# Score banks in pairs, one pair of banks for the maxima, and a new order of the matrix engine's step in a cross-attention kernel

## The chip, the core and the metric

The kernel runs on one core of a Trainium2 chip. The metric is the device time of one execution in microseconds. Engines are named as in the profile: PE (matmul), PEld (weight loads of PE), DVE (vector), ACT (scalar, activations), POOL (GpSimd) and SP (which issues most DMAs).

## The reference

Two layers of a gated network on x of 4 batches x 512 tokens x 512 features: a quantised linear pair (layer 0 attention slot), a mixture of 8 experts with top-2 routing and a shared expert, then a cross-attention with 32 heads of 16 features, and a second mixture of 8 experts. What matters here is the cross-attention and the routing:

```python
q = (x @ Wq).reshape(b, n, 32, 16);  k, v = split(ctx @ Wkv)      # per batch: 512 queries, 512 keys
q, k = rope(q, pos), rope(k, pos)
logits = einsum('bqhd,bkhd->bhqk', q, k) * 0.25
w = softmax(logits, axis=-1)
attn = einsum('bhqk,bkhd->bqhd', w, v)
return attn @ Wout + bout
# router of the first mixture
logits = xt @ gate_w.T          # 512 features to 8 experts
scores = softmax(logits);  top_k(scores + gate_b, 2)
```

## The kernel before

The program is a row of stages: the quantised pair with the keys, values and rotary tables beside it (0 to 297 us of the profile), the first mixture's router with its shared expert (299 to 448), its expert tiles (458 to 693), the attention (697 to 1382), the second mixture (to the end).

**Router.** Per batch, 4 matmuls over the feature chunks c accumulate the 8 x 512 logits in one PSUM bank (L803, 8 of the 128 columns of the array in use, float32: two records each), then four small transposes (L809). **Expert tiles.** `moe.tiles` tiles of 128 rows (40 here), each gathered, multiplied and stored, in a loop over groups of 8.

**Attention.** The work is in 16 units (b, c): batch b, chunk c of 8 heads. q and k are held as sums of bfloat16 parts, so that one bf16 matmul over 6 slots of 16 rows gives a product of float32 quality: Q6 and K6 hold 96 such rows for 8 heads, and three more rows (K: ones, Q: the parts of minus the row maximum) which subtract the maximum inside the score matmul. A turn of unit (b, c) has 8 steps; step s serves heads 4(s//4) to 4(s//4)+3 and key tile s%4. PE's step is written out by hand: `scores` (L1991) of heads 0 and 1, `maxima` (L2004), a slot for a job, `scores` of heads 2 and 3, `maxima`, `values` of the step before (L2016), another slot.

- `scores` writes one head's 128 keys x 512 queries to PSUM bank 4 or 5. `exps` on ACT (L2078) reads that bank and writes E; so a bank comes free for head h+2 after the exp of head h.
- `maxima` runs for a later unit (one or two units ahead): q x k for one head with queries on the partitions, two query tiles at a time, into banks 0, 1 or 2, 3 in turn. DVE reduces the two banks to the maxima `top` (L2217). A pair of banks is free again two pairs later: `pe.wait_ge(maxed, n_max(unit, h, pair) - 2)`.
- `values` takes four heads on four column groups of the array at once, V as weights, into bank 6.
- 16 slots per turn hold the jobs that use bank 7: q projection ("q"), x transposes ("x"), output projection ("p"), transposes of the maxima ("m", L1941), of the sums ("o", L1947) and of the attention rows ("a"). `jobs` gives the slots: q at 0, o at 4 and 11, a at 8, m at 10 of every unit; p and x in the turns c = 0 (slots 12 to 15) and c = 1 (slots 0 and 2).
- DVE runs its 16 reductions per turn, and after reduction n the tasks of slot n (statistics, normalisation, `cut_max` after 7, the shuffle of q after 2, the products of "o" and "p").
- The maxima of a unit go: DVE `cut_max`, PE "m", ACT copy to mT, POOL store to DRAM (L1912) and, when that has landed, POOL load into the three rows of Q6 (L1917); the first `scores` of the unit waits for this load.
- SP loads K6 with 6 DMAs (L1875), stores the parts of q, and loads Q6 with 6 DMAs (L1883). At the stage's start ACT fills the rows of ones with 4 copies (L2040).

Before unit 0 a prologue of turns with b = -1 does the first two q projections, then the maxima of unit 0 (16 reductions) and of half of unit 1 without scores beside them.

## Time and profile before

| | |
|---|---|
| median of 3 runs | 1527.67 us (1524.57 to 1527.68) |
| profiled execution | 1527.5 us, span 1526.0 us |
| PE busy | 1236.6 us (81%) |
| DVE busy | 845.2 us (55%) |
| ACT busy | 635.1 us (42%) |
| POOL busy | 392.8 us (26%) |
| mean granted clock | 0.905 |

Busy time is the time in which an engine had an instruction in work; it says nothing of which engine another waits for. The rows of the timeline and of the groups, further down, give that. A granted clock of 1.00 is the array's 2.4 GHz, 0.50 is 1.2 GHz.

### The profile page before, as it was taken

What the parts mean: (1) busy time and instruction counts of PE and PEld (TensorE: products, weight loads), DVE (VectorE), ACT (ScalarE), POOL (GpSimd) and SP (SyncE); (2) the same over time, 40 slices, a digit from 0 to 9 for tenths busy, and PEclk for the clock granted to TensorE, in tenths of its full rate; (3) what the DMA queues carried; (4) which work ended last, traced back from release to release, by engine and by line L of the source; (5) the groups of instructions that cost most, each with busy time, mean ns of one, the idle gap of its engine ahead of it and who ended that gap; (6) DMA issues with size and microseconds to landing.
All of it is one profiled execution on the core that took longest, in us unless ns stands there. A gap on an engine that the chain in (4) does not pass through costs nothing. (4 is left out here: it accounts for less than half of the span.)

```text
span 1526.0 us, 17989 instructions
## 1 busy us (share of the span) xinstructions
PE 1236.6 (81%) x5318; PEld 542.9 (36%) x5319; DVE 845.2 (55%) x1312; ACT 635.1 (42%) x1136; POOL 392.8 (26%) x459
## 2 busy tenths in 40 slices
PE   2757666499969999991376999999989999975897
PEld 2333333255534444440111323333333333222453
DVE  4585766631424555512385777766756776505544
ACT  1333232345532222224004565555645664742543
POOL 0505143201022222203632332222312330004332
PEclk8778787799999999996657999999999999997999
DMA  5142220243434444427384454433523541007001
GB/s 193 42 139 77 87 99 25 97 166 110 152 104 148 139 159 146 136 72 220 88 152 76 89 92 81 81 68 67 91 57 67 93 87 21 3 1 84 28 35 49
DMA packets 102990, 141.98 MB, mean 93 GB/s; under 512 B 17284, under 2 KB 72068, under 8 KB 102872
## 3 DMA queue, kind: packets, MB, share of 16 engines
q1 hardware_dynamic: 84984, 112.02, 29.2%
q0 software_dynamic: 17936, 29.11, 7.2%
q8 instruction: 34, 0.56, 0.2%
q14 instruction: 36, 0.29, 0.1%
HBM read 97.70 MB, written 46.53 MB: 95 GB/s over the span
## 5 line engine op out<-in xcount | busy, mean ns | idle before, releaser
L2217 DVE TENSOR_REDUCE a_top<-PS 128x2 f32<-128x1024 f32 x256 | 309.8, 1221 | 144.9 <-PE PS L2004 139.6
L2078 ACT ACTIVATE a_E<-PS 128x512 f32<-128x512 f32 x512 | 277.7, 596 | 156.8 <-PE PS L1991 155.4
L1991 PE MATMUL PS<-a_Q,a_K 99*128 99x512 bf16 x512 | 172.0, 388 | 37.3 <-ACT a_E L2078 13.9
L2004 PE MATMUL PS<-a_K,a_Q 96*128 96x512 bf16 x512 | 162.7, 402 | 31.2 <-DMA a_Q<-a_q_parts 19.1
L1252 PE MATMUL PS<-f_W,f_GT 128*128 x320 | 144.6, 595 | 0.0
L2016 PE MATMUL PS<-a_E,a_V 128*32 128x512 f32 x1024 | 139.6, 618 | 0.0
L1991 PEld LDWEIGHTS PS<-a_Q,a_K 99*128 99x128 bf16 x512 | 41.6, 97 | 205.3 <-ACT a_E L2078 164.5
L1323 DVE TENSOR_TENSOR f_H<-f_SG,PS 128x256 f32<-128x256 f32 x40 | 16.8, 421 | 129.7 <-ACT f_SG L1298 129.7
L2004 PEld LDWEIGHTS PS<-a_K,a_Q 96*128 96x128 bf16 x512 | 48.8, 100 | 91.6 <-DVE a_top L2217 27.4
L1252 PEld LDWEIGHTS PS<-f_W,f_GT 128*128 128x128 f32 x320 | 58.1, 192 | 58.2 <-issue 58.2
L1660 POOL TENSOR_TENSOR a_qf<-a_qf,a_tab 128x512 f32<-128x512 f32 x16 | 20.7, 1294 | 212.2 <-DVE a_swapped L2168 212.2
L1271 PE MATMUL PS<-f_W,f_HT 128*128 x160 | 75.1, 593 | 0.0
L1936 PE MATMUL PS<-a_xT,a_wq 128*128 128x512 f32 x128 | 64.1, 648 | 3.7 <-ACT a_xT L2051 3.0
L1957 PE MATMUL PS<-a_wo,a_attnT 128*128 128x512 f32 x128 | 60.4, 616 | 3.4 <-DVE X L2209 2.6
L1298 ACT ACTIVATE f_SG<-PS 128x256 f32<-128x256 f32 x40 | 15.4, 384 | 112.1 <-PE PS L1252 112.1
L2538 PE MATMUL PS<-f_W,f_xb 128*128 128x512 bf16 x256 | 61.9, 386 | 0.0
L825 PE MATMUL PS<-f_W,f0r_xT 128*128 128x512 f32 x128 | 58.3, 598 | 0.0
L1370 POOL DMA_INDIRECT a_rows<-f_y,l_pos x32 | 35.6, 1112 | 65.6 <-POOLq L54 40.2
L2328 POOL TENSOR_TENSOR f_H<-f_HF,f_gates 128x512 bf16<-128x512 f32 x32 | 33.4, 1045 | 71.5 <-DVE f_HF L2409 71.5
L1304 ACT COPY f_Y<-PS 128x512 f32<-128x512 f32 x40 | 23.5, 587 | 62.1 <-PE PS L1271 62.1
L1216 POOL DMA_INDIRECT f_G<-f_xn,f_idx x40 | 40.6, 1015 | 30.2 <-POOL f_idx L1213 30.2
L1213 POOL COPY f_idx<-f_token_of 128x1 int32 (+1 forms) x40 | 15.0, 374 | 128.5 <-PE PS L1232 121.3
(345 smaller groups left out, 1972.3 us busy)
## 6 DMA issues: line engine op xcount, KB each, us to landing
f0r_raw<-in_L_ffn_W_dram SPq DMA_DIRECT2D x24, 512.0 KB, 5.2
a_K<-k_parts SPq DMA_DIRECT2D x96, 128.0 KB, 4.9
a_Q<-a_q_parts SPq DMA_DIRECT2D x96, 128.0 KB, 4.5
f_y<-f_Y SPq DMA_DIRECT2D x40, 256.0 KB, 2.0
v_units<-V SPq DMA_DIRECT2D x16, 512.0 KB, 3.1
a_V<-v_units SPq DMA_DIRECT2D x16, 512.0 KB, 6.3
k_parts<-f_k_parts SPq DMA_DIRECT2D x16, 384.0 KB, 3.4
a_q_parts<-a_parts SPq DMA_DIRECT2D x16, 384.0 KB, 2.6
```

The lines of the kernel that those rows point to most:

```text
L825: last = nc.tensor.matmul(PS[:, 5, 0:2 * I], xT[b % 2][:, c, t * P:(t + 1) * P], W13[:, E, c, :], start=(c == 0), stop=(c == DC - 1))
L1216: pool.indirect_dma_start(out=G[k][:], out_offset=None, in_=xn_dram, in_offset=bass.IndirectOffsetOnAxis(ap=idx[:, k:k + 1].bitcast(U32), ...
L1252: last = nc.tensor.matmul(PS[:, 2 + k % 2, 0:2 * I], GT[k][:, c, :], W13[:, bass.ds(e, 1), c, :].rearrange("p a n -> p (a n)"), start=(c = ...
L1271: last = nc.tensor.matmul(PS[:, 6 + k % 2, :], HT[k][:, c, :], W2[:, bass.ds(e, 1), c, :].rearrange("p a n -> p (a n)"), start=(c == 0), s ...
L1936: last = nc.tensor.matmul(B, wq[:, d, c * P:(c + 1) * P], xT[:, d, :], start=(d == 0), stop=(d == DC - 1))
L1957: last = nc.tensor.matmul(B, attnT[:, d, extra * P:(extra + 1) * P], wo[:, d, :], start=(d == 0), stop=(d == DC - 1))
L1991: nc.tensor.matmul(PS[:, 4 + h % 2, :], K6[k][:, head, kt * P:(kt + 1) * P], Q6[k][:, head, :], start=True, stop=True).then_inc(st_done, 1)
L2004: last = nc.tensor.matmul(PS[:, t, :], Q6[k][0:KR, h, t * P:(t + 1) * P], K6[k][0:KR, h, :], start=True, stop=True)
L2016: last = nc.tensor.matmul(PS[32 * h:32 * h + 32, 6, :], V[k][:, kt, (step // 4) * 4 + h, :], E[step % 2][:, h, :], start=(kt == 0), stop=( ...
L2078: nc.scalar.activation(E[step % 2][:, h, :], PS[:, 4 + h % 2, :], ACT.Exp).then_inc(exp_done, 1)
L2217: nc.vector.tensor_reduce(top[:, h, 2 * pair:2 * pair + 2], PS[:, 2 * pair:2 * pair + 2, :], AX.X, ALU.max).then_inc(maxed, 1)
L2538: last = nc.tensor.matmul(PS[:, 2 * h + m, :], xb[b % 2][:, c, t * P:(t + 1) * P], W13[:, c, m, h * HE:(h + 1) * HE, :].rearrange("p e i - ...
```

## The change

Several edits are joined.

1. Q6 and K6 become [128, 2, 4, 512]: even heads (o = 0) keep slots in rows 0 to 95 and the three rows at 96; odd heads (o = 1) have slots 0 to 3 in rows 64 to 127, slots 4 and 5 in rows 0 to 31, the three rows at 32, and zeros in rows 35 to 63. Each load of K6, of Q6 and of the three rows is split in two (12, 12 and 2 DMAs for 6, 6 and 1). ACT fills the ones and the zeros with 16 instructions.
2. `maxima` uses only the first four slots, 64 rows, and takes two heads at once: even head on rows 0 to 63 into bank 0, odd head on rows 64 to 127 into bank 1. Every pair uses these two banks, and waits for the reduction just before it.
3. `scores` writes two heads to a pair of banks (2, 3 or 4, 5); one exp reads 128 x 1024. A pair of banks is free again a whole step later.
4. PE's step: scores of all four heads, `maxima`, slot, `values`, `maxima`, slot.
5. The first mixture's router puts the four chunks on four column groups (32 columns each) and adds them up in the turning matmul with a matrix `pick`.
6. `moe.tiles` is 39 instead of 40; the last group of the loop is written out.

```diff
-        self.tiles = -(-(2 * self.NT + experts - 1) // (2 * UNROLL)) * 2 * UNROLL
+        self.tiles = 2 * self.NT + experts - 1
...
+            for c in range(DC):
+                if c == 0:
+                    last = nc.vector.tensor_copy(pick[:], identf[:, 0:E])
...
                 for c in range(DC):
                     pe.wait_ge(xT_ready, b * DC + c + 1)
-                    last = nc.tensor.matmul(PS[0:E, 4, :], rwT[:, c, :], xT[b % 2][:, c, :], start=(c == 0), stop=(c == DC - 1))
+                    last = nc.tensor.matmul(PS[32 * c:32 * c + 32, 4, :], rwT[:, c, :], xT[b % 2][:, c, :], start=True, stop=True)
...
                 for i, part in enumerate(Q_PART):
-                    sp.dma_start(Q6[k][i * HEAD:(i + 1) * HEAD], q_parts[...]...).then_inc(q_loaded[k], 16)
+                    for o in range(2):
+                        at = ROWS[o][i]
+                        sp.dma_start(Q6[k][at.start:at.stop, o], by_head[o]).then_inc(q_loaded[k], 16)
...
-                    if not (is_first(unit) and step == 0 and h < 2):
-                        pe.wait_ge(exp_done, n_st(unit, step, h) - 2)
-                    nc.tensor.matmul(PS[:, 4 + h % 2, :], K6[k][:, head, kt * P:(kt + 1) * P], Q6[k][:, head, :],
-                                     start=True, stop=True).then_inc(st_done, 1)
+                    if not (is_first(unit) and step == 0):
+                        pe.wait_ge(exp_done, n_st(unit, step, pair) - 2)
+                    both = (step // 4) * 2 + pair
+                    for o, rows_ in enumerate((MAX_AT[0] + 3, P)):
+                        last = nc.tensor.matmul(PS[:, 2 + 2 * pair + o, :], K6[k][0:rows_, o, both, kt * P:(kt + 1) * P],
+                                                Q6[k][0:rows_, o, both, :], start=True, stop=True)
+                    last.then_inc(st_done, 1)
...
-                    if not (is_first(unit) and h == 0):
-                        pe.wait_ge(maxed, n_max(unit, h, pair) - 2)
-                    for t in range(2 * pair, 2 * pair + 2):
-                        last = nc.tensor.matmul(PS[:, t, :], Q6[k][0:KR, h, t * P:(t + 1) * P], K6[k][0:KR, h, :], start=True, stop=True)
+                    if not (is_first(unit) and h == 0 and pair == 0):
+                        pe.wait_ge(maxed, n_max(unit, h, pair) - 1)
+                    t = 2 * (h % 2) + pair
+                    for o in range(2):
+                        at = slice(o * FOUR, (o + 1) * FOUR)
+                        last = nc.tensor.matmul(PS[:, o, :], Q6[k][at, o, h // 2, t * P:(t + 1) * P], K6[k][at, o, h // 2, :],
+                                                start=True, stop=True)
                     last.then_inc(scored, 1)
...
                     scores((b, c), step, 0)
                     scores((b, c), step, 1)
                     maxima(*heads[step], 0)
                     slot(2 * step)
-                    scores((b, c), step, 2)
-                    scores((b, c), step, 3)
-                    maxima(*heads[step], 1)
                     if step == 0:
                         values(before(b, c, 1), 7)
                     else:
                         values((b, c), step - 1)
+                    maxima(*heads[step], 1)
                     slot(2 * step + 1)
...
-                    exps((b, c), step, (0, 1))
+                    exps((b, c), step, 0)
+                    exps((b, c), step, 1)
                     slot(2 * step)
-                    exps((b, c), step, (2, 3))
```

How this moves PE's instructions is seen best in steps 5 and 6 of a unit. PE before; L1991 are scores, L2004 maxima, L1941 the job "m", L2016 values, L1947 the job "o":

```order
L1991 MATMUL PS<-a_Q6_2,a_K6_2 128x512 x2
L2004 MATMUL PS<-a_K6_0,a_Q6_0 128x512 x2
L1941 MATMUL PS<-identb,a_mcut 24x128 x4
L1991 MATMUL PS<-a_Q6_2,a_K6_2 128x512 x2
L2004 MATMUL PS<-a_K6_0,a_Q6_0 128x512 x2
L2016 MATMUL PS<-a_E0,a_V2 32x512 x4
L1947 MATMUL PS<-identf,a_OT 128x128 x4
L1991 MATMUL PS<-a_Q6_2,a_K6_2 128x512 x2
```

PE of the changed kernel at the same place; L1986 are scores, L2004 again maxima, L1934 "m", L2017 values, L1940 "o":

```order
L1986 MATMUL PS<-a_Q6_2,a_K6_2 128x512 x4
L2004 MATMUL PS<-a_K6_0,a_Q6_0 128x512 x2
L1934 MATMUL PS<-identb,a_mcut 24x128 x4
L2017 MATMUL PS<-a_E0,a_V2 32x512 x4
L2004 MATMUL PS<-a_K6_0,a_Q6_0 128x512 x2
L1940 MATMUL PS<-identf,a_OT 128x128 x4
L1986 MATMUL PS<-a_Q6_2,a_K6_2 128x512 x4
```

The four scores stand together; the two pairs of maxima have only the values (and a job) between them on one side, and only the scores (and a job) on the other.

ACT at the start of the attention, before: the rows of ones, then the table load and the square root of the first normalisation (a_sd).

```order
L2040 COPY a_K6_0<-ones_b 3x4096
L2040 COPY a_K6_1<-ones_b 3x4096
L2040 COPY a_K6_2<-ones_b 3x4096
L2040 COPY a_K6_3<-ones_b 3x4096
L2092 ACT_TABLE_LOAD
L2092 ACTIVATE a_sd<-a_mv,ln_eps 128x4
```

ACT of the changed kernel: the first four of sixteen such rows; the same four follow for buffers 1, 2 and 3, and then the table load and a_sd.

```order
L2039 COPY a_K6_0<-ones_b 3x2048
L2042 ACTIVATE a_Q6_0<-ones_b 32x2048
L2042 ACTIVATE a_K6_0<-ones_b 32x2048
L2045 COPY a_K6_0<-ones_b 3x2048
L2039 COPY a_K6_1<-ones_b 3x2048
```

Four instructions of half the length took the place of each one.

## Rows read from the trace of the kernel before

**Rows 1.** Groups of instructions: busy us, mean ns | idle before, releaser.
```profile
L2217 DVE TENSOR_REDUCE a_top<-PS 128x2 f32<-128x1024 f32 x256 | 309.8, 1221 | 144.9 <-PE PS L2004 139.6
L2078 ACT ACTIVATE a_E<-PS 128x512 f32<-128x512 f32 x512 | 277.7, 596 | 156.8 <-PE PS L1991 155.4
...
L2203 DVE TENSOR_TENSOR a_attn<-PS,a_rsum 128x256 f32<-128x256 f32 x32 | 13.6, 424 | 1.3
```
**Rows 2.** Timeline of PE, one plain step: start us, length us, instruction, count, idle before.
```profile
1026.04 0.60 PE L1991 MATMUL PS<-a_Q,a_K 99*128 99x512 bf16 x2
1026.48 0.60 PE L2004 MATMUL PS<-a_K,a_Q 96*128 96x512 bf16 x2
...
1027.91 0.60 PE L2004 MATMUL PS<-a_K,a_Q 96*128 96x512 bf16 x2
1028.44 1.06 PE L2016 MATMUL PS<-a_E,a_V 128*32 128x512 f32 x8
1029.44 0.61 PE L1991 MATMUL PS<-a_Q,a_K 99*128 99x512 bf16 x2
...
1030.31 3.60 PE L1936 MATMUL PS<-a_xT,a_wq 128*128 128x512 f32 x8
```
**Rows 3.** Timeline of DVE: reduction 7, the one after `cut_max`, and two plain ones.
```profile
1014.28 1.23 DVE L2217 TENSOR_REDUCE a_top<-PS 128x2 f32<-128x1024 f32 x1 [0.20 <-PE PS L2004]
...
1016.74 2.35 DVE L2217 TENSOR_REDUCE a_top<-PS 128x2 f32<-128x1024 f32 x2
...
1027.12 1.22 DVE L2217 TENSOR_REDUCE a_top<-PS 128x2 f32<-128x1024 f32 x1 [0.74 <-PE PS L2004]
```
**Rows 4.** Timeline in the prologue, where PE waits for the reductions.
```profile
784.09 5.82 DVE L2217 TENSOR_REDUCE a_top<-PS 128x2 f32<-128x1024 f32 x5
...
785.35 0.60 PE L2004 MATMUL PS<-a_K,a_Q 96*128 96x512 bf16 x2 [1.14 <-DVE a_top L2217]
```
**Rows 5.** Timeline: first scores of three units, and POOL's load of the maxima.
```profile
946.87 0.60 PE L1991 MATMUL PS<-a_Q,a_K 99*128 99x512 bf16 x2 [0.31 <-DMA a_Q<-a_m_rows]
...
992.90 0.60 PE L1991 MATMUL PS<-a_Q,a_K 99*128 99x512 bf16 x2
...
1057.92 0.51 POOL L1917 DMA_DIRECT2D a_Q<-a_m_rows  x1 [4.92 <-DMA a_m_rows<-a_mT]
...
1061.57 0.60 PE L1991 MATMUL PS<-a_Q,a_K 99*128 99x512 bf16 x2 [1.15 <-DMA a_Q<-a_m_rows]
```
**Rows 6.** Timeline of PE in the last unit: two steps without maxima.
```profile
1332.02 0.88 PE L1991 MATMUL PS<-a_Q,a_K 99*128 99x512 bf16 x2 [0.47 <-ACT a_E L2078]
...
1334.90 0.88 PE L1991 MATMUL PS<-a_Q,a_K 99*128 99x512 bf16 x2 [0.47 <-ACT a_E L2078]
```
**Rows 7.** Timeline of the prologue: ACT's fills, its square root, SP's loads, DVE, first scores.
```profile
696.76 14.11 ACT L2040 COPY a_K<-ones_b 3x4096 bf16<-3x4096 bf16 x4 [3.31 <-PEq L54]
...
724.40 0.30 ACT L2092 ACTIVATE a_sd<-a_mv,ln_eps 128x4 f32<-128x4 f32 x1 [12.23 <-DVE a_mv L2139]
...
753.39 2.69 SPq L1883 DMA_DIRECT2D a_Q<-a_q_parts  x6
...
764.46 3.58 DVE L2217 TENSOR_REDUCE a_top<-PS 128x2 f32<-128x1024 f32 x3 [12.13 <-PE PS L2004]
...
789.94 0.20 DVE L2179 TENSOR_SCALAR a_ntop<-a_top 128x32 f32<-128x32 f32 x1
...
811.14 1.04 PE L1991 MATMUL PS<-a_Q,a_K 99*128 99x512 bf16 x2 [9.32 <-DMA a_Q<-a_m_rows]
```
**Rows 8.** Busy time by stretch: PE, PEld, DVE, ACT, POOL, granted clock, DMA share, GB/s.
```profile
766.00:769.00 3.00, 2.71 (x6) 0.26 (x4) 2.96 (x4) 0.00 (x0) 0.00 (x0) 0.50 1.04 313
...
1325.00:1350.00 25.00, 20.57 (x114) 5.55 (x113) 1.36 (x4) 20.07 (x39) 1.05 (x2) 1.00 0.01 3
```
**Rows 9.** The router's matmuls of the last batch (timeline); the expert tiles' first matmuls (line).
```profile
384.98 3.60 PE L803 MATMUL PS<-f0r_xT,f0r_rwT 128*8 128x512 f32 x8
...
L1252 PE MATMUL PS<-f_W,f_GT x320: 592/592/1061, 460.5 to 686.6; 128*128 x160
```

More of the change, by code:

```diff
@@ L678, in add @@
                     nc.vector.tensor_tensor(X[:, j, :], X[:, j, :], Z[j % TB][:], ALU.add).then_inc(added, 1)
+            for c in range(DC):
+                if c == 0:
+                    last = nc.vector.tensor_copy(pick[:], identf[:, 0:E])
+                else:
+                    v.wait_ge(pick_ready, c)
+                    last = nc.vector.tensor_tensor(pick[:], pick[:], identf[:, c * 32:c * 32 + E], ALU.add)
+                last.then_inc(pick_ready, 1)
             for b in range(NB):
@@ L807, in logit @@
                 pe.wait_ge(lT_ready, b + 1)
+                pe.wait_ge(pick_ready, DC)
                 for t in range(TB):
-                    last = nc.tensor.transpose(PS[:, 4, t * E:(t + 1) * E], lT[:, t * P:(t + 1) * P], identf[0:E, 0:E])
+                    last = nc.tensor.matmul(PS[:, 4, t * E:(t + 1) * E], lT[:, t * P:(t + 1) * P], pick[:], start=True, stop=True)
                 last.then_inc(l_turned, 1)
@@ L1142, in expert_tiles @@
         GT = [sb(f"GT{k}", [P, DC, P], dt) for k in range(U)]
-        H13 = [sb(f"H13_{k}", [P, 2 * I], dt) for k in range(U)] if narrow else None
         SG = [sb(f"SG{k}", [P, I], dt) for k in range(U)]
@@ L1183, in peeled @@
                     turn(group, i, lambda lag: 0 <= group * G + i - lag < T)
-            def looped(first, end):
-                with eng.Fori(first, end) as group:
-                    for i in range(G):
-                        turn(group, i, lambda lag: True)
+            assert T // G >= key_work.NB
             peeled(0, G)
-            if beside:
-                looped(1, key_work.NB)
-                for group in range(key_work.NB, T // G):
-                    peeled(group, G)
-            else:
-                looped(1, T // G)
-            peeled(T // G, deepest)
+            with eng.Fori(1, T // G) as group:
+                for i in range(G):
+                    turn(group, i, lambda lag: True)
+            peeled(T // G, T % G + deepest)
         def nth(j, k, unit):
@@ L1222, in _ @@
         def _(pe):
-            tb = 1 if dt == F32 else 2
             def turn_x(j, k):
@@ L1834, in n_max, with n_st @@
             return b * (DC * HU * 2) + c * HU * 2 + h * 2 + pair + 1
-        def n_st(unit, step, h):
+        def n_st(unit, step, pair):
             b, c = unit
-            return b * (DC * 32) + c * 32 + step * 4 + h + 1
+            return b * (DC * 16) + c * 16 + step * 2 + pair + 1
         block = s.enter_context(nc.Block())
@@ L1915, in turn @@
                     pool.wait_ge(pv_done, n_unit(unit, 8) - RING * 8)
+                else:
+                    pool.wait_ge(ones_ready, 4 * RING)
                 pool.nop(nofuse=True)
-                pool.dma_start(Q6[unit[1]][KR:KR + 3], row.rearrange("a (i h) s -> i (a h) s", i=3)).then_inc(m_loaded, 16)
+                by_head = row.rearrange("a (i h o) s -> o i (a h) s", i=3, o=2)
+                for o in range(2):
+                    pool.dma_start(Q6[unit[1]][MAX_AT[o]:MAX_AT[o] + 3, o], by_head[o]).then_inc(m_loaded, 16)
             turns(pool, turn)
```

150 lines of the change are left out of this document (75 added, 75 removed).

## Prediction

> **What bounds the kernel now.** I read the groups of instructions first, then the timeline of one plain step on PE and DVE, then the starts of units, the prologue and the tail. The groups [rows 1] show two engines that seem to wait for PE: DVE, 309.8 us of reductions with 144.9 us of idle time before them, and ACT, 277.7 us of exps with 156.8. Neither is full. In the plain step [rows 2] scores begin at 1026.04 and again at 1029.44: 3.40 us. Of this PE streams 4 scores and 4 maxima of about 0.22 each and the values, 1.00 (1028.44 to 1029.44), some 2.75; the rest are its waits for an exp before the second pair of scores. So the loop between two score banks and ACT costs about 0.6 us a plain step, and the double-buffered maxima cost nothing.
>
> **The half-step after the change.** Four banks let the exps run a step behind: PE no longer waits for them. But now every pair of maxima waits for the reduction just before it, and that reduction waits for its matmuls. The loop has four pieces. (a) From the first matmul of a pair to the reduction: 1026.48 to 1027.12, 0.64 [rows 2, 3], with two matmuls behind each other; if the two run side by side, 0.22 less, 0.43. (b) The reduction, 1.22 [rows 1]. (c) From its end to the next matmul: the reduction that starts at 784.09 ends at 785.31, PE starts at 785.35 [rows 4]: 0.04. (d) nothing else. Sum 1.70 per half-step, 3.40 per step. PE's own work between is smaller: maxima 0.22, a gap of 0.09 (values start 0.53 behind the maxima, where two matmuls take 0.44), values 1.00, together 1.3; on the other side 0.22 + 0.09 + four scores 0.87 + 0.09, about 1.3. So a plain step takes 3.40 after as before: **the bound moves from the exps to the reductions, and the step gains nothing.** PE's 0.4 us of slack per half hides short transposes (0.44); the long projection (3.44, from 1030.31 [rows 2]) makes its half 4.85, DVE standing idle meanwhile.
>
> That the halves run side by side is an assumption with bounds: the nearest row is the values, whose four matmuls of 32 columns take 1.00 together [rows 2] while the projection's four full ones take 3.44. The loop has 0.43 or 0.64 in it; I take 0.43. The Trainium skill (TensorEngine Tiling (Array Packing), Tiling Modes) says the same of row groups of 64, and also that a change of tiling mode drains the array, which speaks against this change: maxima in a mode of their own make four changes a step instead of two. The row prices one change at 0.09; by it the two added ones lie in halves that have 0.4 us of slack, so they cost nothing; were that slack absent, 2 x 0.09 x 128 steps would be 23 us.
>
> **What the loop costs in a unit.** Before, a vector task between reductions was hidden by the second pair of banks. Now it delays the next reduction by its length less 0.48 (the refill). cut_max: reduction 7 ends at 1015.51, the next starts at 1016.74 [rows 3], 1.23, so +0.75. The two "o" tasks (0.42 [rows 1] and a reciprocal, about 0.7 with their gaps) +0.25 each, the shuffle (estimate 0.75) +0.3, transposes that overflow the slack +0.15: 1.7 per unit. A unit of chunk 2 or 3 is then 4.85 + 15 x 1.70 + 1.7 = 32.05. Before: 1029.44 [rows 2] to 1061.57 less its wait of 1.15 [rows 5], 30.98. So **+1.1**. Chunk 1 with its three short jobs, two projections: 7.8 + 1.7 + 4.85 + 13 x 1.70 + 1.4 = 37.9, against 992.90 to 1029.44 [rows 5, 2], 36.5: **+1.4**. Chunk 0, with three output projections: 4.85 + 11 x 1.70 + 4.85 + 1.70 + 4.85 + 6.15 + delays 4.6 (statistics and normalisation too, an estimate) = 45.7, against 946.87 to 992.90, 46.0: **-0.3**; there PE's wait for ACT's table loads goes.
>
> **The maxima's transfer.** The chain m, copy, store, load is already late: scores at 1061.57 waited 1.15 us, at 946.87 0.31 [rows 5]. It now has less time. From the job in slot 10 to the next unit's scores: before 9.9 us, after 1.4 + 1.95 + 3 x 1.70 + 0.3 = 8.75, and 0.4 of lateness hides in the loop: 0.75 less. And it is longer: a second load on POOL behind the first (0.51 [rows 5]), and mT's copy behind both exps (0.25). So 1.5 us later in chunk 2 and 3, 0.3 after chunk 1, none after chunk 0 where projections cover it. Sum per batch: 3.3. With the units above, 2 x 1.1 + 1.4 - 0.3 + 3.3 = 6.6; rounded down, since batches differ, **+6.2 for each of batches 0, 1, 2**. Batch 0 also adds rows on DVE in each unit (1.5 us, an estimate, hidden before): 4 x 1.0, **+4**. Batch 3: three of its units lose 4 in all.
>
> **The tail.** 12 steps have no maxima. They take 2.88 now, with 0.47 waiting for an exp [rows 6]. After, an exp of 1024 elements bounds it: between 0.60 (no more than one of 512) and 1.19 (two of 596 [rows 1]); I take 1.0, nearer the two, since the elements stay and only one start is saved. PE's values stand between the scores, so the cycle is about 2.1: 12 x 0.75, some -9, of which 3.5 goes back to the maxima's transfer of the last unit, for which 2.5 short steps are too few: **-5**. The Trainium skill (ScalarE: Activation LUTs, What ACT_TABLE_LOAD costs) gives 186 ns + 0.833 ns an element less an overlap of 93, 0.95; by it the tail is 0.5 us shorter. Batch 3 together: **-1**.
>
> **The prologue** [rows 7]. Four fills took 14.11; sixteen of half the length take about 29.6 (3.53 halved, and a little more for the fixed part). The square root behind them began at 724.40, as its input came; now the fills end at 726.4 and a table load of about 1.3 follows: **+3.6** for everything to the first maxima. SP's Q6 loads: 2.69 for six, 5.4 for twelve, last data **+2**. Then 16 reductions stand between 764.46 and 789.94: 25.5, of which 16 x 1.16 [rows 4] is theirs. The clock is at 1.2 GHz there [rows 8], a single matmul takes 0.6 (1.04 for two, less 0.43), so a half is 0.61 + 0.04 + 1.22 + 0.05 = 1.92: 30.7 instead of 18.6, less about 1 hidden: **+11**. The job m stands three maxima later: **+1.6**. From m to the first scores at 811.14 took 16.7 us, because 2 MB of other loads share the DMA engines; they now come at another time: **-4**. Sum +14.2.
>
> **Before the attention.** Each router group of matmuls took 3.60 [rows 9]; on four column groups it should take what the values take, 1.06: 4 x 2.54, less DVE's four small pick instructions at the start (0.6, an estimate from the smallest vector rows, 0.2 as at 789.94 [rows 7], in a chain): **-9.6**; PE is full after, so this counts. One tile of 40 goes: (686.6 - 460.5)/40 [rows 9], **-5.7**.
>
> **Sum.** -9.6 - 5.7 + 14.2 + 3 x 6.2 + 4 - 1 = +20.5 on the profiled execution's 1527.5 (the median of the runs is 1527.67, the same): **1548 us**.
>
> **Rivals.** *The last unit's gain everywhere, the other side:* the loop is shorter than my four pieces say, because PE has its weights loaded and the release comes before the reduction's recorded end. It decides at a half-step of 1.61: some 230 halves are bound by the loop, 0.1 us on each is 23 us. At 1.60, with the transfer covered by the slack thus regained, 1548 - 23 - 10 = 1515. For it: DVE and PE rows are rounded and their ends modelled. Against it: the distances in [rows 3, 4] are between recorded starts. Chance 0.16. *The pairs of maxima don't overlap* (the change doesn't do what it says): 0.21 x 230 = +48, 1596. Chance 0.10. *The clock falls.* PE streams 2.2 of 3.4 us where it streamed 2.75. In the prologue 2.71 busy of 3.00 stood at 0.50; in the tail 20.57 of 25 kept 1.00 [rows 8], and there the streaming share is 1.87 of 2.88, 65%, as in the new step. That speaks for 1.00. At 1.2 GHz a half is PE's 2.5 us: 0.8 x a third of 230, +60, 1608. Chance 0.08. *It cancels:* the prologue's +14 hides in DMA waits and the time is 1527. Chance 0.06.
>
> **How the numbers follow.** A measurement tells 0.2%, 3 us, from no change. The forecast, 0.60, spans 1532 to 1565 for its unknown prices: exp, fills, transfer. The range takes most of both outer rivals: 1518 to 1592. Faster 0.16, within 0.2% 0.07 (the cancelling case and the edge of my own), slower 0.77.
>
> **What would show it.** Right: reductions 1.70 apart in plain halves, with idle time before the maxima ending in the reduction; almost no idle time before scores from an exp; first scores some 14 us later relative to the stage's start; waits of 2 to 3 us for the load of maxima before units of chunk 3 and 0; router matmuls of about 1 us. Wrong: plain steps well under 3.3 us, or reductions 1.9 apart, or a granted clock under 0.95 in the units.

## The result, and the profile after

The changed kernel takes **1537.82 us** (median of 4 runs, 1537.13 to 1539.43) against 1527.34 (4 runs, 1524.57 to 1527.68): ratio 1.0074, 95% interval 1.0057 to 1.0092, so 10.5 us slower. The forecast was 1548.0, with a range of 1518 to 1592. The profiled execution took 1538.25 us, with a span of 1536.8 beside 1526.0.

The page of the changed kernel, groups of instructions (busy us, mean ns | idle before, releaser) and DMA issues (count, KB each, us to landing):

```profile
L2223 DVE TENSOR_REDUCE a_top<-PS 128x2 f32<-128x1024 f32 x256 | 313.5, 1225 | 172.5 <-PE PS L2004 168.1
L2082 ACT ACTIVATE a_E<-PS 128x1024 f32<-128x1024 f32 x256 | 248.2, 1022 | 167.8 <-PE PS L1986 114.8
L2004 PE MATMUL PS<-a_K,a_Q 64*128 64x512 bf16 x512 | 105.6, 409 | 122.5 <-DVE a_top L2223 102.3
...
a_K<-k_parts SPq DMA_DIRECT2D x192, 64.0 KB, 2.2
a_Q<-a_q_parts SPq DMA_DIRECT2D x192, 64.0 KB, 2.2
```

Beside [rows 1] the reductions are as long as before (1225 ns against 1221), but DVE is idle for 172.5 us ahead of them instead of 144.9. The exps are half as many and cost 30 us less, on an engine that was not the bound. PE now idles 102.3 us ahead of maxima, for a reduction. The last two rows were not forecast: a load of 128 KB took 4.9 us (K) and 4.5 (Q) to land before; each of the two halves takes 2.2.

PE and DVE over three halves and the start of a unit of chunk 2 (compare [rows 2, 3]):

```profile
1031.26 0.39 PE L2004 MATMUL PS<-a_K,a_Q 64*128 64x512 bf16 x2 [0.52 <-DVE a_top L2223]
1031.59 1.04 PE L1986 MATMUL PS<-a_Q,a_K 99*128 99x512 bf16 x3
1032.98 0.39 PE L2004 MATMUL PS<-a_K,a_Q 64*128 64x512 bf16 x2 [0.35 <-DVE a_top L2223]
1033.30 1.07 PE L2017 MATMUL PS<-a_E,a_V 128*32 128x512 f32 x8
1034.69 0.39 PE L2004 MATMUL PS<-a_K,a_Q 64*128 64x512 bf16 x2 [0.33 <-DVE a_top L2223]
1035.02 1.05 PE L1986 MATMUL PS<-a_Q,a_K 99*128 99x512 bf16 x4
1036.41 0.39 PE L2004 MATMUL PS<-a_K,a_Q 64*128 64x512 bf16 x2 [0.34 <-DVE a_top L2223]
```
```profile
1033.41 1.23 DVE L2223 TENSOR_REDUCE a_top<-PS 128x2 f32<-128x1024 f32 x1 [0.49 <-PE PS L2004]
1035.13 1.23 DVE L2223 TENSOR_REDUCE a_top<-PS 128x2 f32<-128x1024 f32 x1 [0.49 <-PE PS L2004]
1036.84 1.23 DVE L2223 TENSOR_REDUCE a_top<-PS 128x2 f32<-128x1024 f32 x1 [0.49 <-PE PS L2004]
```

Maxima start 1.71 to 1.72 us apart, each pair behind the reduction before it: 0.43 from the matmul to the reduction (1036.41 to 1036.84), 1.22 of reduction, 0.06 back. Two matmuls on two row groups take 0.39 together, as one does, so they run side by side. In these plain halves DVE idles 0.49 and PE 0.33 to 0.35. There is no wait for an exp in these rows.

Where the time went, by marks that both traces have (us):

| stretch | before | after | difference | forecast |
|---|---|---|---|---|
| start to the first expert matmul | 460.5 | 454.0 | -6.5 | -9.6 |
| expert tiles | 226.1 | 221.4 | -4.7 | -5.7 |
| to the first transposes of x | 40.4 | 44.7 | +4.3 | +3.6 |
| to the first scores | 84.1 | 87.2 | +3.1 | +10.6 |
| batch 0 | 135.7 | 140.7 | +5.0 | +10.2 |
| batch 1 | 146.1 | 151.0 | +4.9 | +6.2 |
| batch 2 | 144.9 | 149.9 | +5.0 | +6.2 |
| batch 3, to the start of its last output projection | 139.9 | 136.0 | -3.9 | -1 |
| second mixture (not touched) | 148.2 | 152.0 | +3.9 | 0 |

The last row belongs to neither kernel. It is counted from the start of the last output projection. From the start of the last matmul of that projection the code is the same in all kernels here; counted so, the profile of before shows 145.1 us, after 148.9, and the twelve experiments 146.6 to 148.7. The granted clock tells them apart. Busy time by stretch (PE, PEld, DVE, ACT, POOL, granted clock, DMA share, GB/s), the same place in before and after:

```profile
1441.00:1461.00 20.00, 18.11 (x108) 9.50 (x109) 9.29 (x18) 9.83 (x15) 7.75 (x9) 1.00 0.08 27
```
```profile
1448.00:1468.00 20.00, 17.47 (x97) 8.93 (x99) 9.40 (x18) 9.84 (x15) 7.18 (x9) 0.91 0.08 28
```

Before has 1.00 there, after 0.91. So it is in all fourteen profiles: the five with 145.1 to 147.3 us show 1.00 in this stretch, the nine with 147.9 to 148.9 show 0.91, whatever their attention. Over the whole mixture the granted clock was 0.93 in before and 0.88 in after. It follows none of the edits. Whether it differs between executions of one kernel is not shown, since each kernel has one profile; but one profile of each is no ground for 3 us in a stretch that nothing changed.

### The profile page after: what moved, and what is told of

The parts are those of the page before. It is cut to its first block and busy times, and to the rows that moved or that the text cites. A ratio compares the mean times of both kernels' runs of the same rounds, so it can differ in the third digit from the quotient of the medians.

```text
span 1536.8 us, 17627 instructions
## 1 busy us (share of the span) xinstructions
PE 1179.3 (77%) x5253; PEld 520.2 (34%) x5317; DVE 846.6 (55%) x1314; ACT 626.6 (41%) x889; POOL 400.6 (26%) x474
## 5 line engine op out<-in xcount | busy, mean ns | idle before, releaser
L2223 DVE TENSOR_REDUCE a_top<-PS 128x2 f32<-128x1024 f32 x256 | 313.5, 1225 | 172.5 <-PE PS L2004 168.1
L2082 ACT ACTIVATE a_E<-PS 128x1024 f32<-128x1024 f32 x256 | 248.2, 1022 | 167.8 <-PE PS L1986 114.8
L2004 PE MATMUL PS<-a_K,a_Q 64*128 64x512 bf16 x512 | 105.6, 409 | 122.5 <-DVE a_top L2223 102.3
L2017 PE MATMUL PS<-a_E,a_V 128*32 128x512 f32 x1024 | 139.2, 611 | 0.4 <-ACT a_E L2082 0.4
L1986 PE MATMUL PS<-a_Q,a_K 128*128 128x512 bf16 (+1 forms) x469 | 131.9, 384 | 4.1 <-DMA a_Q<-a_m_rows 0.9
L2004 PEld LDWEIGHTS PS<-a_K,a_Q 64*128 64x128 bf16 x512 | 25.0, 93 | 294.3 <-DVE a_top L2223 247.4
L1929 PE MATMUL PS<-a_xT,a_wq 128*128 128x512 f32 x128 | 69.8, 695 | 3.7 <-ACT a_xT L2056 3.0
L1986 PEld LDWEIGHTS PS<-a_Q,a_K 99*128 99x128 bf16 (+1 forms) x512 | 41.4, 98 | 64.2 <-issue 23.1
L1901 POOL DMA_DIRECT2D a_m_rows<-a_mT x16 | 9.2, 577 | 165.8 <-ACT a_mT L2067 165.8
L2062 ACT ACTIVATE a_qf<-PS 128x512 f32<-128x512 f32 x16 | 9.6, 598 | 97.2 <-PE PS L1929 86.9
```

The costliest lines, as they stand in the source:

```text
L1929: last = nc.tensor.matmul(B, wq[:, d, c * P:(c + 1) * P], xT[:, d, :], start=(d == 0), stop=(d == DC - 1))
L1986: last = nc.tensor.matmul(PS[:, 2 + 2 * pair + o, :], K6[k][0:rows_, o, both, kt * P:(kt + 1) * P], Q6[k][0:rows_, o, both, :], start=True ...
L2004: last = nc.tensor.matmul(PS[:, o, :], Q6[k][at, o, h // 2, t * P:(t + 1) * P], K6[k][at, o, h // 2, :], start=True, stop=True)
L2017: last = nc.tensor.matmul(PS[32 * h:32 * h + 32, 6, :], V[k][:, kt, (step // 4) * 4 + h, :], E[step % 2][:, h, :], start=(kt == 0), stop=( ...
L2082: nc.scalar.activation(E[step % 2][:, 2 * pair:2 * pair + 2, :], PS[:, 2 + 2 * pair:4 + 2 * pair, :], ACT.Exp).then_inc(exp_done, 1)
L2223: nc.vector.tensor_reduce(top[:, h - h % 2:h - h % 2 + 2, t], PS[:, 0:2, :], AX.X, ALU.max).then_inc(maxed, 1)
```

## The experiments

Times are medians; a ratio is to the kernel before on the same chip, with its 95% interval. The experiments ran on several chips, on which the kernel before took 1526.0 to 1528.6 us, so a difference between two experiments can be a few us off.

**Router and tiles alone** (e6): the changed kernel with the attention of before.

```diff
-        def n_st(unit, step, pair):
+        def n_st(unit, step, h):
...
                     slot(2 * step)
+                    scores((b, c), step, 2)
+                    scores((b, c), step, 3)
+                    maxima(*heads[step], 1)
                     if step == 0:
...
-                    maxima(*heads[step], 1)
                     slot(2 * step + 1)
```

> The changed kernel with its attention put back to that of before: the router on column groups and 39 tiles stay. My accounting of the two traces says that these parts brought 6.5 us before the experts and 4.7 us in the tiles, so the time is 11.2 us under before: ratio 0.9927. It also tells what the 3.9 us in the second mixture are, whose code the change does not touch. If they come with the changed attention (its lower share of streaming matmuls, or an earlier end of its work on another engine), the second mixture takes 148.2 us here as before, and the granted clock in its first 20 us is that of before. Rival: they come with the shift in time or with the shorter tiles; then the mixture takes about 152 us here too and the gain is 7 us, ratio 0.995.

Measured: 1518.2 us, ratio 0.9945 (0.9932 to 0.9958), 8.4 us under before by the ratio, 9.4 by the medians. The tiles take 221.6 us, -4.5. The first expert matmul comes at 456.5. Over all profiles it comes at 458.0 to 460.5 with the old router (4 profiles, mean 459.3) and at 453.4 to 456.5 with the new (10, mean 454.6): the router brings 4.7 us, and the 6.5 of the table were partly chance. The second mixture took 150.4 us from the start of the last output projection, between the two theories (148.2 and 152): 2.2 of the 3.9 are there without the changed attention. So these two parts brought some 8 to 9 us and **the attention costs about 19**.

The router was forecast by the row of the values (1.06 for four column groups). Timeline of PE in the changed kernel, the router's matmuls of the last batch and what follows:

```profile
380.34 2.14 PE L814 MATMUL PS<-f0r_xT,f0r_rwT 128*32 128x512 f32 x8
382.42 3.70 PE L837 MATMUL PS<-f_W,f0r_xT 128*128 128x512 f32 x8
```

2.08 us from one to the other, where [rows 9] had 3.53: -1.45 for each of four batches, 5.8. Each matmul waits for its own copy of x, made by ACT in 0.60; whether that spacing keeps the four from running together was not tried.

**Two banks for the maxima in the kernel before** (e7).

```diff
-                    if not (is_first(unit) and h == 0):
-                        pe.wait_ge(maxed, n_max(unit, h, pair) - 2)
+                    if not (is_first(unit) and h == 0 and pair == 0):
+                        pe.wait_ge(maxed, n_max(unit, h, pair) - 1)
-                        last = nc.tensor.matmul(PS[:, t, :], ...
+                        last = nc.tensor.matmul(PS[:, t - 2 * pair, :], ...
-                        ... PS[:, 2 * pair:2 * pair + 2, :], AX.X, ALU.max)
+                        ... PS[:, 0:2, :], AX.X, ALU.max)
```

> The kernel before with one thing changed: the maxima go through two PSUM banks instead of four, so that each pair of matmuls waits for the reduction of the pair before. By my loop (0.64 from the first of two matmuls behind each other to the reduction, 1.22 reduction, 0.04 back) a half takes 1.90 and a plain step 3.80 instead of 3.40: over some 112 plain steps 45 us, with the tasks of VectorE no longer hidden some 10 to 15 more: ratio 1.036 to 1.040. This is also the case 'the pairs do not overlap' of my forecast with the old exps. Rival: the loop is shorter than its pieces, since the matmuls are issued ahead and the exps set the pace; then the plain step stays at 3.4 and the ratio is under 1.01.

Measured: 1587.88 us, ratio 1.0394 (1.0374 to 1.0413). Timeline of PE:

```profile
1058.94 0.60 PE L2004 MATMUL PS<-a_K,a_Q 96*128 96x512 bf16 x2
1059.65 0.88 PE L1991 MATMUL PS<-a_Q,a_K 99*128 99x512 bf16 x2
1060.86 0.60 PE L2004 MATMUL PS<-a_K,a_Q 96*128 96x512 bf16 x2 [0.32 <-DVE a_top L2217]
1061.39 1.07 PE L2016 MATMUL PS<-a_E,a_V 128*32 128x512 f32 x8
1062.39 0.61 PE L1991 MATMUL PS<-a_Q,a_K 99*128 99x512 bf16 x2
1062.83 0.60 PE L2004 MATMUL PS<-a_K,a_Q 96*128 96x512 bf16 x2
```

1.92 and 1.97 a half, 3.89 a step (1058.94 to 1062.83) against 3.80 by the sum of the pieces. This is the cost of one pair of banks without the pairing of matmuls: +60 us, from an edit of the banks alone. The rival with the shorter loop falls.

**The banks given back** (e2): changed kernel, four maxima banks and two score banks with one exp a head, PE's order of before; row groups, split loads and fills stay.

```diff
-                    if not (is_first(unit) and h == 0 and pair == 0):
-                        pe.wait_ge(maxed, n_max(unit, h, pair) - 1)
+                    if not (is_first(unit) and h == 0):
+                        pe.wait_ge(maxed, n_max(unit, h, pair) - 2)
...
                     slot(2 * step)
+                    scores((b, c), step, 2)
+                    scores((b, c), step, 3)
+                    maxima(*heads[step], 1)
                     values((b, c), step - 1)
-                    maxima(*heads[step], 1)
                     slot(2 * step + 1)
```

> The changed kernel with the banks given back: four for the maxima in turn, as before, two for the scores with one exp a head, and PE's order of before (scores, scores, maxima, scores, scores, maxima, values). What stays is the maxima on two row groups side by side. If the single pair of maxima banks is what binds the changed kernel, the reductions are no longer tied to their own matmuls, and the bound is the loop of scores and exps as before: 3.40 less at most one pair's 0.22 us that the second maxima no longer stream between scores and values, so 3.2 to 3.4 a step, and the time is 10 to 35 us under the changed kernel: ratio to before 0.985 to 1.000. Rival: the time went into the longer prologue, the split loads and ScalarE, not into the banks; then the ratio stays at 1.005 to 1.010.

Measured: **1494.91 us, ratio 0.9772 (0.9745 to 0.98)**: 34 us under before and 43 under the changed kernel, more than the range expected. Timeline of PE:

```profile
1020.02 0.88 PE L1986 MATMUL PS<-a_Q,a_K 99*128 99x512 bf16 x2 [0.23 <-ACT a_E L2084]
...
1021.15 1.07 PE L2016 MATMUL PS<-a_E,a_V 128*32 128x512 f32 x8
...
1023.01 0.66 PE L1945 MATMUL PS<-identf,a_attn 128*128 128x128 f32 x4
...
1024.44 1.07 PE L2016 MATMUL PS<-a_E,a_V 128*32 128x512 f32 x8
```

Values start 3.29 us apart, and a short job (L1945) fits in without lengthening the step. A unit's eight steps without an output projection take 30.1 (from values to values), in the changed kernel 32.0, in e1b below, which is before without its waits at unit starts, 30.9. The prologue gains too: first maxima to first scores 38.5 us, after 52.0, before 47.7. So the bank swap (one pair for the maxima, two pairs with long exps for the scores, and the order that goes with them) costs more than all the rest brings, as the theory says. This run takes the three back together; that the number of maxima banks is what costs is shown by e7 and by e8 below. It also shows that **the row groups were worth having**, 0.8 us a unit against e1b, once the banks did not pay for them.

**The values between the halves** (e3): as e2, the values moved from behind the second maxima to behind the first slot.

```diff
                     slot(2 * step)
+                    values((b, c), step - 1)
                     scores((b, c), step, 2)
                     scores((b, c), step, 3)
                     maxima(*heads[step], 1)
-                    values((b, c), step - 1)
```

> As the version with four banks for the maxima, and the values of the step before stand between the two halves: scores, scores, maxima, values, scores, scores, maxima. The exps of the first two scores then run under the values (1.0 us), so that PE does not wait for them. PE streams 0.88 scores, 0.4 maxima and 1.0 values with changes of mode, some 2.6 us; ScalarE has four exps of 0.60, 2.4; VectorE two reductions of 1.22, 2.44. I expect a plain step of 2.7 to 3.0 us instead of 3.42, over some 112 steps 45 to 80 us: ratio to before 0.95 to 0.98. Rival: the transfer of the maxima (the row must be through DRAM and back within the last steps of a unit) or the DMA loads bind as soon as the steps are shorter; then plain steps are short but waits of some us stand at the starts of units, ratio 0.98 to 1.0. A second: PE's changes of tiling mode cost more than 0.09 each and the step is 3.2 or more.

Measured: 1511.73 us, ratio 0.9885 (0.986 to 0.991), 17 us worse than e2. A plain step is 3.21 us, not 2.7 to 3.0. My reasoning was wrong: there is one group of values in a step, so seen as a ring the order is the same. The pair of scores behind the values never waits and the other always does; moving the values only changes which pair that is. The wait did not go, and the stretch with the output projections grew (the eight steps from values to values that hold them: 54.7 against 50.9), the other units a little too (30.6 against 30.1). Some of this is the clock: in this profile the q projection of chunk 1 took 5.39 us in batches 1 and 2 with the granted clock at 0.50 (977 to 980), where e2's took 3.70, 1.7 us each.

**Maxima one bank at a time** (e8): changed kernel, each matmul waits for its own bank's reduction, 512 reductions of 512 elements. `n_max` counts two reductions a pair here.

```diff
+                        if not (is_first(unit) and h == 0 and pair == 0):
+                            pe.wait_ge(maxed, n_max(unit, h, pair) - 3 + o)
-                    last.then_inc(scored, 1)
+                        nc.tensor.matmul(PS[:, o, :], ...).then_inc(scored, 1)
...
+                        for o in range(2):
+                            v.wait_ge(scored, n_max(unit, h, pair) - 1 + o)
+                            nc.vector.tensor_reduce(top[:, h - h % 2 + o:h - h % 2 + o + 1, t], PS[:, o:o + 1, :], AX.X, ALU.max).then_inc(maxed, 1)
```

> The changed kernel (four score banks, one exp over a pair) with its two banks for the maxima used one at a time: each matmul of a pair waits for the reduction of its own bank alone, and VectorE reduces 512 elements in each of 512 instructions instead of 1024 in 256. If the loop 'matmuls, reduction over both banks, matmuls' is what binds, cutting it in two lets VectorE reduce one bank while PE fills the other. VectorE then has four reductions a step: between half of 1.22 each (2.44) and half plus 0.1 for a second start (2.84); PE has some 2.8 of its own. I expect a plain step of 2.9 to 3.1 us instead of 3.42, and 35 to 55 us under the changed kernel: ratio to before 0.97 to 0.985. Rival: VectorE is bound by its starts, a reduction of 512 takes 0.8 us or more and the step 3.3 or more: ratio 1.00 to 1.01.

Measured: 1514.87 us, ratio 0.9922 (0.9899 to 0.9944), 23 us under the changed kernel, less than expected. Its group of reductions, and DVE in two plain steps:

```profile
L2223 DVE TENSOR_REDUCE a_top<-PS 128x1 f32<-128x512 f32 x512 | 327.1, 685 | 131.7 <-PE PS L2004 123.8 <-issue 2.8 <-DVE a_mcut L2191 0.3
```
```profile
1015.85 2.61 DVE L2223 TENSOR_REDUCE a_top<-PS 128x1 f32<-128x512 f32 x4
1018.92 2.63 DVE L2223 TENSOR_REDUCE a_top<-PS 128x1 f32<-128x512 f32 x4 [0.46 <-PE PS L2004]
```

A reduction of 512 takes 0.685 by the group and 0.65 in a row, and the plain step is 3.07. Cutting the loop in two works in plain steps, but a unit falls only from 32.0 to 30.3 and the stretch with the output projections hardly (54 us): with two banks, every DVE task and every PE job still stands between a reduction and its refill. Four banks can hide these, which fits e2's 50.9 for the same stretch; e2 also has the old exps and the old order, so this last step is argued.

**The loads cut in two, in the kernel before** (e1b). The layout stays; `o` is even or odd heads, and Q6 is treated alike.

```diff
-                    sp.dma_start(K6[k][i * HEAD:(i + 1) * HEAD], ...)
+                    for o in range(2):
+                        sp.dma_start(K6[k][i * HEAD:(i + 1) * HEAD].rearrange("r (h o) s -> r o h s", o=2)[:, o], ...)
```

> The kernel before with each load of K6 and Q6 cut in two, over the even and the odd heads; the layout in SBUF stays, so that each destination row is written in four pieces of 1 KB. Versions with the new layout and twice as many loads all show landings of 2.2 us for K and Q, with the changed steps or with nearly the old ones; kernels with the old loads show 4.3 to 4.9. Theory: the cut alone makes them land sooner, so they do here too, 2.2 to 2.6 us, and the time falls by the waits at the starts of units, 0 to 4 us: ratio 0.997 to 1.000. Rival: the shorter landing comes from the new layout (each destination row written in one piece of 4 KB); then they stay at 4 us or more here and the time is as before or up to 3 us longer.

Measured: **1516.9 us, ratio 0.9932 (0.9914 to 0.995)**: 10 us faster than before by an edit that adds instructions to SP's queue, more than either theory said. Landings: 2.8 us for K and Q (before: 4.9 and 4.5; after: 2.2), so the cut alone brings most of it. DMA issues of before and of this kernel in their prologues (792 to 812 and 791 to 804), us to landing:

```profile
a_K<-k_parts SPq DMA_DIRECT2D x6, 128.0 KB, 7.9
...
a_m_rows<-a_mT POOLq DMA_DIRECT2D x1, 24.0 KB, 5.1
a_Q<-a_m_rows POOLq DMA_DIRECT2D x1, 24.0 KB, 9.1
```
```profile
a_K<-k_parts SPq DMA_DIRECT2D x11, 64.0 KB, 4.9
...
a_m_rows<-a_mT POOLq DMA_DIRECT2D x1, 24.0 KB, 3.0
```

SP issues one DMA in some 0.46 us whatever its size ([rows 7]: six in 2.69; here twelve in 5.48), so the same bytes are issued over twice the time. Busy time, granted clock (0.50 in both), DMA share and GB/s in four us around the store of the row (at 796.30 and 795.19), first before, then this kernel:

```profile
797.00:801.00 4.00, 2.27 (x5) 0.39 (x6) 4.00 (x5) 0.00 (x0) 0.00 (x0) 0.50 1.16 133
```
```profile
796.00:800.00 4.00, 2.38 (x5) 0.40 (x6) 4.00 (x5) 0.00 (x0) 0.93 (x2) 0.50 0.55 144
```

The DMA share is the time that the packets begun there took, over the time of the 16 engines, so that it can pass 1. The bytes moved in a us are no fewer with the halves (144 GB/s against 133), but their packets take half the engines' time. POOL's small transfer then passes sooner: over the kernel the store of the row of maxima lands in 3.2 us instead of 4.8. Whether it passes through gaps between the issues, or because a half load costs the engines less for each byte, these rows do not tell apart.

First maxima to first scores takes 40.8 us instead of 47.7, and in batches 1 and 2 eight steps without an output projection take 30.9 everywhere, where before takes 30.9 to 32.1. That excess is the stall of the transfer, which I had forecast to grow. Chunk 0 of batches 1 and 2 is 1.0 us shorter too, but there the profile of before has the granted clock at 0.50 (964 to 967, and again 1111 to 1113) and this one has not.

**Late fills** (e4, e5, e9): the sixteen fills moved behind the first copies of q, first maxima not waiting for them; on the changed kernel, on e3 and on e8.

```diff
-            for k in range(RING):
-                nc.scalar.copy(K6[k][MAX_AT[0]:MAX_AT[0] + 3, 0]...
...
                     slot(2 * step)
+                    if isinstance(b, int) and b == -1 and c == 2 and step == 0:
+                        fill()
```

> The changed kernel with ScalarE's sixteen fills of the K and Q buffers moved from the start of the attention to behind the first copies of q, and the first maxima no longer waiting for them (they read none of those rows). By the trace the fills held the first matmul on x back by 4.3 us. If all of that is on the path, the time is 4 us under the changed kernel, ratio to before 1.0048. Rival: the fills now stand in front of the copies of q for the next units or of the row of maxima, and the first scores, which wait for that row at the end of the prologue, come at the same time as in the changed kernel: ratio 1.007.

> Values between the halves and four banks for the maxima, and the late fills as well. The sum of the two if both work: 4 us under the version with early fills. If the first scores do not depend on the fills, the same time as that version within 0.2%.

> Maxima one bank at a time and the late fills. The late fills brought 7 us to the changed kernel and 5 to 7 us to the version with the values between. If they do the same here, 5 to 7 us under the version with early fills. If the shorter half-steps in the prologue leave the fills less cover, 0 to 4 us.

Measured: e4 1530.99 us, ratio 1.0022 (1.0011 to 1.0032), 6.8 under the changed kernel; e5 1507.05, 0.9864 (0.9837 to 0.9891), 4.7 under e3; e9 1507.14, 0.987 (0.9846 to 0.9894), 7.7 under e8. In e4 last expert matmul to first transpose of x takes 39.0 us; after took 44.7 and before 40.4, so before's own four fills (14.11 us) cost about 1.4. ACT in the changed kernel and in e4:

```profile
714.25 1.90 ACT L2045 COPY a_K<-ones_b 3x2048 bf16<-3x2048 bf16 x1
716.16 1.28 ACT L2097 ACT_TABLE_LOAD   x1
717.46 0.30 ACT L2097 ACTIVATE a_sd<-a_mv,ln_eps 128x4 f32<-128x4 f32 x1
```
```profile
711.56 0.30 ACT L2096 ACTIVATE a_sd<-a_mv,ln_eps 128x4 f32<-128x4 f32 x1 [24.60 <-DVE a_mv L2145]
```

All of it was on the path; with the fills first, even the table load stood on it, which in e4 runs at 685.68, long before the square root's input comes.

**e2 with late fills** (e10), and on top of it **both pairs of maxima together** (e11):

```diff
                     maxima(*heads[step], 0)
+                    maxima(*heads[step], 1)
                     slot(2 * step)
                     scores((b, c), step, 2)
                     scores((b, c), step, 3)
-                    maxima(*heads[step], 1)
                     values((b, c), step - 1)
```

> Four banks for the maxima, two for the scores, PE's order of before, maxima on two row groups, and the late fills: the sum of two measured edits, 0.9772 to before less 5 to 7 us, some 1488 us, ratio 0.973. If the fills are covered by something else there, 0.977.

> Four banks for the maxima, two for the scores, late fills, and PE's order changed: both pairs of maxima between the first and the second pair of scores (scores, scores, maxima, maxima, slot, scores, scores, values). In the version without this the plain step is 3.28 us and the second pair of scores waits 0.2 to 0.4 us for the exp of the first: 1.15 us pass from the first score to the second pair, of which PE works about 0.75. The second pair of maxima (0.33) fills that wait, and two changes of tiling mode go. I expect 2.85 to 3.05 us a plain step, 25 to 45 us under the version without it: ratio to before 0.945 to 0.96. Rival: the wait moves elsewhere, as it did when the values were put between the halves: behind the long projection or to the reductions (2.45 us a step and VectorE's own tasks); then 0 to 10 us, ratio 0.97 to 0.975.

Measured: e10 1491.01, 0.9758 (0.9734 to 0.9782); e11 **1481.22 us, 0.9709 (0.9688 to 0.9731)**, the fastest of the study, 44 us (2.9%) under before. Plain steps fall to 2.96 as expected:

```profile
1023.92 1.07 PE L2014 MATMUL PS<-a_E,a_V 128*32 128x512 f32 x8
1024.91 0.61 PE L1986 MATMUL PS<-a_Q,a_K 99*128 99x512 bf16 x2
1025.45 0.60 PE L2001 MATMUL PS<-a_K,a_Q 64*128 64x512 bf16 x4
1026.07 0.88 PE L1986 MATMUL PS<-a_Q,a_K 99*128 99x512 bf16 x2
1026.88 1.06 PE L2014 MATMUL PS<-a_E,a_V 128*32 128x512 f32 x8
...
1048.28 0.39 PE L2001 MATMUL PS<-a_K,a_Q 64*128 64x512 bf16 x2 [0.74 <-DVE a_top L2225]
```

but a unit falls only from 30.1 to 29.0, and the time by 9.8 us, not 25 to 45: steps with a DVE task take 3.1 to 3.9 now, waiting for reductions as in the last row, since DVE needs 2.45 for two reductions and has its own tasks beside them (`cut_max` puts 1.23 between two reductions, [rows 3]). "112 plain steps" was too many: in a unit of chunk 2 or 3 only two of the eight steps take 2.96.

**The same order in the kernel before** (e12).

> The kernel before with PE's order alone changed in the same way: scores, scores, maxima, maxima, slot, scores, scores, values. My reading of before was that its plain step of 3.40 us holds 0.6 us of waits for an exp and 2.75 us of work. If so, the second pair of maxima (0.44) covers the wait and the step is 2.85 to 3.0: over 112 plain steps 45 to 60 us less, some of it lost to the maxima's transfer, which then has less time: ratio 0.965 to 0.98. Rival: the wait for the exp is not the bound of the step, but the sum of PE's changes of mode and its work is; then the step stays over 3.3 us and the ratio is 0.995 to 1.0.

Measured: 1524.86 us, ratio 0.9981 (0.9962 to 1.0001): nothing that can be told from zero. PE, two plain steps, and the start of the next unit:

```profile
1025.16 1.07 PE L2016 MATMUL PS<-a_E,a_V 128*32 128x512 f32 x8
...
1028.12 1.07 PE L2016 MATMUL PS<-a_E,a_V 128*32 128x512 f32 x8
...
1060.64 0.88 PE L1991 MATMUL PS<-a_Q,a_K 99*128 99x512 bf16 x2 [1.60 <-DMA a_Q<-a_m_rows]
```

The plain step is 2.96, 0.44 less, so my reading of the exp wait in [rows 2] was right. But where the next unit's row of maxima must arrive, the step with the projection of q takes 9.6 and 10.3 us in batch 1, where before takes 7.5 and 6.8: counted from values to values, the eight steps that hold the starts of chunks 3 and 0 take 33.0 and 33.7 (before: 32.1 and 31.4), and only the eight that hold the start of chunk 2, whose row is early, gain (29.0, before 30.9). Part of it is the clock: behind the wait at 1060.64 the granted clock was 0.50 (1061 to 1064), and the projection there took 4.2 us instead of 3.6. The loads are those of before (4.9 us for K, 4.7 for the row's store). e12 with split loads was not run; that e11 has both and no such wait suggests it, without proving it.

## Why the prediction was right, and where its sum was off

**The mechanism was right.** The bound moved from the exps to the reductions: 1.70 a half forecast, 1.71 to 1.72 measured; the exps no longer bound the step; the pairs overlap; the clock was 1.00 in the units of chunk 2 and 3 (1035 to 1067 us); the prologue's half 1.92 forecast, 1.93 measured (755.31 to 757.24, at 0.50). A unit of chunk 2 was forecast at 32.05 and took 31.97 in batches 1 and 2. e7 and e8 show the loop from either side. The Trainium skill (TensorEngine Tiling (Array Packing), Tiling Modes) lets row groups of 64 run side by side, and the trace agrees: 0.39 us for two. What the added changes of mode cost was not measured; a plain half leaves room for them, since PE waits 0.33 in it.

**The size was 20.5 forecast and 10.5 measured, and the total is closer than its parts.** The terms of the attention add up to 35.8 in the prediction; e6 puts its cost at about 19. The router, too hopeful by 5, and 3.9 us in a stretch that no edit touches hid part of that, which is luck. By terms:
- *"So 1.5 us later in chunk 2 and 3", +3.3 a batch for the maxima's transfer:* wrong in sign, the worst step. I counted the second load on POOL (0.51 forecast, 1.23 for both measured) and the shorter lead, and did not ask what the twelve loads on SP do to the DMA engines. Spread over twice the time they left the engines half as busy, and the transfer got faster. One such wait was left, 0.92 us in the tail. e1b prices the cut at 10 us of gain in the kernel before.
- *Chunk 0 -0.3 and chunk 1 +1.4:* too low, and they hid the first error. In batch 1, first scores to first scores, chunk 0 took 47.3 (46.0 before), chunk 1 39.7 (36.5), chunk 2 32.0 (32.1 with its old wait) and chunk 3 32.0 (31.4). Sum +4.9 a batch against +6.2, so nearly right by two errors of opposite sign. The loop itself was priced well in chunk 1, at 37.9; what came on top is 1.7 us of clock. Timeline of PE there, and busy time, granted clock (0.52 and 1.00), DMA share and GB/s just behind, first after, then before:

```profile
998.47 0.66 PE L1924 MATMUL PS<-identf,a_xh 128*128 128x128 f32 x4 [1.24 <-ACT a_xT L2056]
999.88 5.39 PE L1929 MATMUL PS<-a_xT,a_wq 128*128 128x512 f32 x8 [0.76 <-ACT a_xT L2056]
...
1000.00:1003.00 3.00, 3.00 (x4) 1.17 (x5) 0.00 (x0) 0.00 (x0) 0.00 (x0) 0.52 0.00 0
```
```profile
995.21 0.66 PE L1931 MATMUL PS<-identf,a_xh 128*128 128x128 f32 x4 [0.81 <-ACT a_xT L2051]
996.62 3.69 PE L1936 MATMUL PS<-a_xT,a_wq 128*128 128x512 f32 x8 [0.76 <-ACT a_xT L2051]
...
997.00:1000.00 3.00, 3.00 (x8) 1.24 (x7) 0.00 (x0) 0.00 (x0) 0.00 (x0) 1.00 0.00 0
```

  The same projection takes 5.39 us behind somewhat longer idle times of PE, and 5.39 again in batch 2 (from 1150, at 0.55), against 3.70 in chunks 2 and 3. So the rival "the clock falls" came true in this one place. In chunk 0 of batch 1 both profiles have such a stretch (973 to 976 in after at 0.50, 964 to 967 in before); in batch 2 only before has one, and chunk 0 took 46.0 there, as forecast (45.7).
- *Batch 0 "+4" for rows added by DVE:* they are there, at 0.7 us a unit: chunk 2 takes 32.7 in batch 0 and 32.0 in the later ones. Two such instructions stand between reductions that then start 2.59 apart (873.12 to 875.71) instead of 1.72:

```profile
874.27 0.74 DVE L1363 SCALAR_TENSOR_TENSOR X<-a_rows,a_tw,X 128x512 f32<-128x512 f32 x1
```

  Batch 0 still came to +5.0 like the others, since its chunk 0, which has no output projection, took 38.2 against 40.0 before. Why that one gained was not looked into.
- *Prologue +14.2:* +7.4. The reductions were right (+10.7 against +11), fills +4.3 against +3.6 (the prediction's own rows give 726.4 + 1.3 - 724.40 = 3.3). From the first transposes of x to the first maxima it took 1.2 us less instead of 2 more; the job m was 0.3 late, not 1.6; from m to the first scores 6.4 us went, not 4. The last is again the split loads: in e1b 7.2 go there. The first two are not: in e1b the first maxima come 0.6 later, and m as in before. Their cause stays open.
- *Tail -5:* batch 3 gave -3.9 instead of -1. From the last maxima to the last values it took 30.5 us, before 37.4, so -6.9. The steps gave less than forecast (7.8 instead of 9), since only those without a job took 2.0 to 2.3 and the others 2.5 to 3.6; but the wait for the last unit's row that was to take 3.5 back took 0.9. Another 1.7 us of batch 3 is the clock again: the first of the four output projections took 5.37 in before, at 0.72 (1362 to 1368), and 3.67 in after, at 1.00. The exp of 1024 took 1.022 us by its own length, where I took 1.0, and two behind each other start 0.92 apart. For that distance the Trainium skill (ScalarE: Activation LUTs, What ACT_TABLE_LOAD costs) gives an estimate of 0.95 (186 ns + 0.833 ns an element, less an overlap of 93), and the trace is 0.03 under it.
- *Router -9.6, tiles -5.7:* -4.7 over ten profiles and -4.7. A row of another matmul (1.06) was taken for one that takes 2.08.

So the loop, the sign of the change and the place of the loss stand as predicted. The cost of the transfer does not, and the total of the batches came near by errors that cancel.

## What to carry to other kernels

PSUM banks that go to one loop are taken from another: write both loops down (matmul, reader, refill) before and after, and count the tasks that stand between a reader's end and the refill, because a double-buffered loop hides them and a single one does not. Three edits came joined here: router and tiles (-8), split loads (-10, measured in the kernel before) and the banks (a loss larger than both); joined they read as one small loss, and apart two are worth keeping. An order inside a step is a ring: moving work in it pays only if it comes to stand inside the wait. Before an odd microsecond is put down to the program, read the granted clock of both kernels at that place.

## What was not expected of the hardware

Loads issued by one queue took some 0.46 us each to issue, at 128 KB as at 64 KB. With 128 KB a 24 KB store of another queue landed in 4.8 us; with 64 KB in 3.2, and in 2.3 to 2.5 in the kernels with the new layout. The same bytes kept the DMA engines half as busy (0.55 against 1.16), at 144 and 133 GB/s. Smaller DMAs were the faster program.

The granted clock in an untouched stretch differed from profile to profile (0.91 or 1.00 over 20 us). In the attention it fell to 0.50 for short stretches, in one place behind idle times of PE of 1.24 and 0.76 us, and there a projection of 3.70 us lasted 5.39. Such stretches lie in different places in different kernels, and one of them was worth up to 1.7 us.
